# Scores of twelve tiles in PSUM, and ScalarE scaling a copy for the leaky step, in the plain layers of a graph attention network

## The chip, the cores and the metric

The kernel runs on one core of a Trainium2 chip. The metric is the device time of one execution in microseconds (us). Five engines work side by side: TensorE (PE, matmuls and weight loads), VectorE (DVE), ScalarE (ACT), GpSimd (POOL) and SyncE (SP). They meet only at semaphores: an instruction raises a counter when it ends, another engine waits for a value of it. SBUF is the large on-chip memory; PSUM is the memory that TensorE writes to, in banks of 512 float32 per partition, which DVE and ScalarE can read and write too and GpSimd can't.

## The reference, cut to what matters

12,500 nodes with 64 features and 212,500 edges, sorted by destination. One attention layer with two heads and edge features comes first, then three plain layers, which the change is about. Each of the three computes this (ReLU between them, a residual behind the last):

```python
def _gat_conv(x, src, dst, W, a_src, a_dst, b, n_nodes):
    h = x @ W
    alpha_s = h @ a_src
    alpha_d = h @ a_dst
    e = alpha_s[src] + alpha_d[dst]
    e = jnp.where(e > 0, e, NEG_SLOPE * e)
    m = jax.ops.segment_max(e, dst, num_segments=n_nodes)
    m = jnp.where(jnp.isfinite(m), m, 0.0)
    ex = jnp.exp(e - m[dst])
    s = jax.ops.segment_sum(ex, dst, num_segments=n_nodes)
    alpha = ex / (s[dst] + 1e-16)
    out = jax.ops.segment_sum(alpha[:, None] * h[src], dst, num_segments=n_nodes)
    return out + b
```

NEG_SLOPE is 0.2; the leaky step is max(0.2 e, e).

## The kernel before

A plain layer cuts the edges into units of up to 2048 edges that fall on a window of 128 nodes. A unit is 16 tiles of 128 edges: an edge is a partition of a tile, a node is a column. Its scores are a block of 128 partitions x 16 tiles x 128 nodes, in which only the column of an edge's own node counts; the rest is pushed to about minus 2 to the 80th. Each layer has 116 units. The loop body holds four units (RING), and most buffers exist four times or twice. The order of work on each engine is written out by hand in one function per engine; nothing schedules it. A helper, `step`, makes DVE wait for its own instruction before it goes on (its bookkeeping shows as line 122).

For unit n, line numbers in brackets:

- GpSimd gathers the source rows of tiles 4 to 15, one indirect DMA per tile, twelve a unit (L2149). It waits only for the buffer to be free and for the indices, so that it may run up to three units ahead. Tiles 0 to 3 come from rows near the window, picked out by matmuls with one-hot matrices (L2429, L2433), which DVE makes (the picks, L2220 and L2222).
- TensorE spreads the distance of every edge's destination to every column over four PSUM banks, `ps_apart`, with four matmuls of 512 columns (L2418), and the nodes' own attention term over a row (L2410). DVE turns both into a mask in SBUF (L2204). This is done one unit ahead: the distances of unit n + 2 are spread while unit n is worked on.
- ScalarE writes the scores, one activation per tile, from mask and gathered row into `prob` in SBUF (L2362): tiles 0 to 11, then, when the last gathers have landed, 12 to 15.
- DVE takes the maximum over tiles: tiles 0 to 3 against 4 to 7 (L2276), against 8 to 11 (L2277), and, once all are scored, against 12 to 15 (L2279), then L2280 and L2281 down to one column maximum per node. Two small steps for the running sums follow (L2250, L2255), then the leaky step over the whole block (L2285).
- Meanwhile TensorE transposes the column maximum (L2489), spreads distances, and adds up tiles 8 to 11 of the unit before (L2463). DVE reduces (L2289), applies slope and the running maximum (L2290, L2292); TensorE transposes the result (L2494, L2495). DVE subtracts it from the scores (L2299, three pieces), ScalarE takes the exponential (L2392), TensorE adds up (L2463). The result of the unit two before is projected for the next layer (L2450, ScalarE's copy L2348, L2442), except in the last layer, where it is stored with a residual (L2243).

## Time and profile before

| | us |
|---|---|
| median of 3 runs | 8424.12 (8423.76 to 8430.99) |
| profiled execution, its own time | 8423.76 |
| its span, first to last instruction | 8421.8 |
| busy: DVE | 7298.0 (87%) |
| busy: POOL | 6249.3 (74%) |
| busy: PE | 6174.9 (73%) |
| busy: ACT | 4528.2 (54%) |
| granted TensorE clock, mean | 0.614 of 2.4 GHz |

Busy time is the time in which an engine has an instruction of its own under way; issuing and waiting are not in it. The three plain layers lie from about 2540 us to the end, the two-headed layer and the preparation ahead of them. Shares over the whole span mix these parts, so the rows below are taken from stretches of the plain layers. A releaser, written behind an arrow, is what the profile takes to have ended a wait.

### The profile page before, as it was taken

What the parts mean: (1) busy time and instruction counts of PE and PEld (TensorE: products, weight loads), DVE (VectorE), ACT (ScalarE), POOL (GpSimd) and SP (SyncE); (2) the same over time, 40 slices, a digit from 0 to 9 for tenths busy, and PEclk for the clock granted to TensorE, in tenths of its full rate; (3) what the DMA queues carried; (4) which work ended last, traced back from release to release, by engine and by line L of the source; (5) the groups of instructions that cost most, each with busy time, mean ns of one, the idle gap of its engine ahead of it and who ended that gap; (6) DMA issues with size and microseconds to landing.
All of it is one profiled execution on the core that took longest, in us unless ns stands there. A gap on an engine that the chain in (4) does not pass through costs nothing. (4 is left out here: it accounts for less than half of the span.)

```text
span 8421.8 us, 166392 instructions
## 1 busy us (share of the span) xinstructions
PE 6174.9 (73%) x42912; PEld 5513.0 (65%) x42912; DVE 7298.0 (87%) x15865; ACT 4528.2 (54%) x13224; POOL 6249.3 (74%) x5871
## 2 busy tenths in 40 slices
PE   3666766677766777777777887777776777777777
PEld 3666656666655666666666776666665666666666
DVE  7888888888888888888887888888888888888888
ACT  3777767777754555454554444444444444444444
POOL 5777767777727777777776777777776777777776
PEclk9666666666666656555655556565555555555555
DMA  3222222222222222222222222222222222222222
GB/s 92 51 54 51 52 49 55 51 55 59 57 76 49 38 37 38 37 38 38 37 38 39 37 38 38 37 38 38 37 38 40 41 42 42 41 42 42 41 42 37
DMA packets 599846, 379.87 MB, mean 45 GB/s; under 512 B 435012, under 2 KB 488015, under 8 KB 599478
## 3 DMA queue, kind: packets, MB, share of 16 engines
q0 software_dynamic: 187248, 203.53, 14.9%
q1 hardware_dynamic: 404561, 169.88, 8.9%
q10 hardware_dynamic: 7952, 5.60, 0.2%
q14 instruction: 66, 0.54, 0.0%
q8 instruction: 19, 0.31, 0.0%
HBM read 345.43 MB, written 33.90 MB: 45 GB/s over the span
## 5 line engine op out<-in xcount | busy, mean ns | idle before, releaser
L2149 POOL DMA_INDIRECT plain_rows_in<-table,plain_idx x4176 | 4521.7, 1083 | 1401.9 <-issue 1386.1
L2463 PEld LDWEIGHTS plain_ps_sums<-plain_rows_in,plain_prob 128*128 128x128 f32 x11232 | 2241.0, 297 | 183.6 <-issue 66.0
L2463 PE MATMUL plain_ps_sums<-plain_rows_in,plain_prob 128*128 128x65 f32 x11232 | 2265.9, 381 | 31.0 <-ACT plain_prob L2392 20.8
L2392 ACT ACTIVATE plain_prob<-plain_prob 128x512 f32<-128x512 f32 (+1 forms) x1044 | 795.0, 772 | 2635.2 <-DVE plain_prob L2299 2593.8
L1517 POOL DMA_INDIRECT heads_rows_in<-h_in,heads_idx x1664 | 1702.8, 1023 | 655.0 <-issue 586.5
L2362 ACT ACTIVATE plain_prob<-plain_mask,plain_rows_in 128x128 f32<-128x128 f32 x5568 | 1684.0, 388 | 236.9 <-DMA plain_rows_in<-table,plain_idx 197.6
L2299 DVE TENSOR_TENSOR plain_prob<-plain_prob,plain_ps_max 128x512 f32<-128x512 f32 (+1 forms) x1044 | 841.1, 861 | 321.4 <-PE plain_ps_max L2495 321.4
L2433 PEld LDWEIGHTS plain_ps_out<-plain_pieces,plain_picks 128*128 128x128 bf16 x15795 | 956.2, 136 | 0.0
L2433 PE MATMUL plain_ps_out<-plain_pieces,plain_picks 128*128 128x66 bf16 x15795 | 939.6, 245 | 0.0
L2204 DVE SCALAR_TENSOR_TENSOR plain_mask<-plain_ps_apart,plain_er_rows 128x2048 f32<-128x2048 f32 x351 | 804.5, 2292 | 16.4 <-PE plain_ps_apart L2418 4.3
L2285 DVE SCALAR_TENSOR_TENSOR plain_prob<-plain_prob 128x2048 f32<-128x2048 f32 x348 | 795.8, 2287 | 0.0
L1832 PE MATMUL heads_ps_turn<-ident,heads_onehot 128*128 128x128 f32 x1680 | 346.9, 375 | 565.4 <-ACT heads_pairs_t L1710 434.6
L1758 ACT ACTIVATE heads_masked<-heads_mask,heads_scores_sum 128x128 f32<-128x128 bf16 x2496 | 748.8, 389 | 0.0
L1832 PEld LDWEIGHTS heads_ps_turn<-ident,heads_onehot 128*128 128x128 f32 x1680 | 276.1, 194 | 589.9 <-issue 452.2
L2429 PE MATMUL plain_ps_out<-plain_own,plain_self_pick 128*128 128x66 f32 x702 | 238.8, 444 | 574.0 <-DVE plain_picks L2222 563.0
L2410 PE MATMUL plain_ps_max<-ident,plain_er_wide 128*128 128x128 f32 x354 | 139.7, 395 | 679.1 <-DVE plain_column_max L2281 616.1
L2429 PEld LDWEIGHTS plain_ps_out<-plain_own,plain_self_pick 128*128 128x128 f32 x702 | 175.8, 311 | 637.5 <-DVE plain_picks L2222 312.9
L2418 PE MATMUL plain_ps_apart<-selector,plain_dst_local 128*128 128x512 bf16 x1416 | 575.8, 551 | 0.0
L2410 PEld LDWEIGHTS plain_ps_max<-ident,plain_er_wide 128*128 128x128 f32 x354 | 59.1, 167 | 766.8 <-issue 766.8
L1853 PEld LDWEIGHTS heads_ps_acc<-heads_weighted,heads_onehot 128*128 128x128 f32 x3328 | 535.4, 255 | 14.2 <-issue 14.2
L1853 PE MATMUL heads_ps_acc<-heads_weighted,heads_onehot 128*128 128x130 f32 x3328 | 536.3, 336 | 11.0 <-DVE heads_weighted L1634 11.0
L2222 DVE TENSOR_SCALAR plain_picks<-plain_locs,block_ids 128x384 bf16<-128x384 f16 x1755 | 452.1, 322 | 0.0
(385 smaller groups left out, 9812.4 us busy)
## 6 DMA issues: line engine op xcount, KB each, us to landing
plain_rows_in<-table,plain_idx POOLq DMA_INDIRECT x4176
heads_edges<-in_edge_attr SPq DMA_DIRECT2D x108, 512.0 KB
plain_locs<-arranged_loc SPq DMA_DIRECT2D x360, 128.0 KB
heads_rows_in<-h_in,heads_idx POOLq DMA_INDIRECT x1664
plain_own<-table SPq DMA_DIRECT2D x360, 33.5 KB
table<-plain_out_sb SPq DMA_DIRECT2D x232, 33.5 KB
plain_dst_ids<-arranged_dst SPq DMA_DIRECT2D x360, 8.0 KB
plain_unit_par<-plain_floats SPq DMA_DIRECT2D x360, 1.0 KB
```

Of the source, the lines that this page charges most:

```text
L1517: gp.indirect_dma_start(rows_in[h][:, t, :], None, table[:, :], bass.IndirectOffsetOnAxis(ap=idx[h][:, t:t + 1], axis=0)).then_inc(gathere ...
L1758: ins = ac.activation(tile, mask[:, t, :], ACT.Identity, bias=scores_sum[:, t, hd:hd + 1])
L1832: ins = te.transpose(ps_turn[g % TURN_BANKS][0:NB, t % GROUP * P:(t % GROUP + 1) * P], onehot[h][:, t, :], con.ident[:, :])
L1853: ins = te.matmul(acc_ps, onehot[h][:, t, :], weighted[:, t, :], start=t == 0, stop=t == Q - 1)
L2149: gp.indirect_dma_start(rows_in[h][:, t, :], None, table[:, :], bass.IndirectOffsetOnAxis(ap=idx[h][:, t - KEPT:t - KEPT + 1], axis=0)).th ...
L2204: ve.scalar_tensor_tensor(mask[h % 2][:, :, :], apart, 0.0, bcast(er_rows[:, :], 1, Q), ALU.not_equal, ALU.subtract).then_inc(mask_made, 1)
L2285: step(ve.scalar_tensor_tensor(tile[:, :, :], tile[:, :, :], SLOPE, tile[:, :, :], ALU.mult, ALU.max))
L2299: ve.tensor_tensor(tile[:, cols, :], tile[:, cols, :], bcast(max_row, 1, count), ALU.subtract).then_inc(logits_made, 1)
L2362: ins = ac.activation(prob[h % 2][:, t, :], mask[h % 2][:, t, :], ACT.Identity, bias=rows_in[h][:, t, src_at:src_at + 1], scale=-BIG)
L2392: ac.activation(prob[h % 2][:, cols, :], prob[h % 2][:, cols, :], ACT.Exp).then_inc(weights_made, 1)
L2433: ins = te.matmul(ps_class[:, c + 1, :], picks[h % 2][:, b, c * P:(c + 1) * P], pieces[:, k, c * BLOCKS + b, :], start=b + k == 0, stop=b ...
L2463: ins = te.matmul(sums[h % 2], prob[h % 2][:, t, :], rows_in[slot][:, t, 0:part], start=t == 0, stop=t == Q - 1)
```

## The change

Tiles 0 to 3 are scored as before. The scores of tiles 4 to 15 are written to PSUM instead, over the distances (`scores` is a second name for `ps_apart`; the four banks hold tiles 0 to 3, 4 to 7, 8 to 11 and 12 to 15). DVE takes the maxima out of them with one input in PSUM. The leaky step is split: DVE does tiles 0 to 3 in SBUF as before (512 elements), between the second and the third maximum. For tiles 4 to 15 ScalarE copies the scores, multiplied by the slope, into the mask, which is no longer needed (two copies of 1024 and 512 elements); DVE takes the maximum of copy and scores (1536 elements) into `prob`. Since scores now lie over the distances, ScalarE may write them only when DVE has made the next unit's mask, and TensorE may spread the distances that come after only when DVE has taken the scores: bank 0 is spread where all four were, banks 1 and 2 behind the adding up of tiles 8 to 11 of the unit before, bank 3 behind the projection. Three semaphores are new: `tops_made` (second and third maximum), `shrunk` (copies) and `scores_taken`.

```diff
-                    step(ve.tensor_tensor(top[:, :, :], tile[:, 0:THIRD, :], tile[:, THIRD:2 * THIRD, :], ALU.max))
-                    step(ve.tensor_tensor(top[:, :, :], top[:, :, :], tile[:, 2 * THIRD:3 * THIRD, :], ALU.max))
+                    step(ve.tensor_tensor(top[:, :, :], tile[:, 0:KEPT, :], scores[:, KEPT:2 * KEPT, :], ALU.max))
+                    ve.tensor_tensor(top[:, :, :], top[:, :, :], scores[:, 2 * KEPT:EARLY, :], ALU.max
+                                     ).then_inc(tops_made, 1)
+                    step(ve.scalar_tensor_tensor(tile[:, 0:KEPT, :], tile[:, 0:KEPT, :], SLOPE, tile[:, 0:KEPT, :],
+                                                 ALU.mult, ALU.max))
                     ve.wait_ge(scored, n + 1)
-                    step(ve.tensor_tensor(top[:, :, :], top[:, :, :], tile[:, 3 * THIRD:Q, :], ALU.max))
+                    ve.wait_ge(tops_made, 2 * n + 1)
+                    ve.tensor_tensor(top[:, :, :], top[:, :, :], scores[:, EARLY:Q, :], ALU.max).then_inc(tops_made, 1)
+                    ve.wait_ge(tops_made, 2 * n + 2)
                     step(ve.tensor_tensor(top[:, 0:2, :], top[:, 0:2, :], top[:, 2:4, :], ALU.max))
...
                     make_shift(i + (h == RING - 1), after(h))
-                    step(ve.scalar_tensor_tensor(tile[:, :, :], tile[:, :, :], SLOPE, tile[:, :, :],
-                                                 ALU.mult, ALU.max))
+                    ve.wait_ge(shrunk, 2 * n + 2)
+                    ve.tensor_tensor(tile[:, KEPT:Q, :], mask[h % 2][:, KEPT:Q, :], scores[:, KEPT:Q, :], ALU.max
+                                     ).then_inc(scores_taken, 1)
...
                     ve.wait_ge(max_turned, n + 1)
+                    ve.wait_ge(scores_taken, n + 1)
...
                     for t in tiles:
-                        ins = ac.activation(prob[h % 2][:, t, :], mask[h % 2][:, t, :], ACT.Identity,
+                        raw = prob[h % 2] if t < KEPT else scores
+                        ins = ac.activation(raw[:, t, :], mask[h % 2][:, t, :], ACT.Identity,
                                             bias=rows_in[h][:, t, src_at:src_at + 1], scale=-BIG)
...
                         score(h, range(0, KEPT))
+                        ac.wait_ge(mask_made, n + 2)
...
                         score(h, range(EARLY, Q)).then_inc(scored, 1)
+                        ac.wait_ge(scored, n + 1)
+                        for k, cols in enumerate((slice(KEPT, EARLY), slice(EARLY, Q))):
+                            ac.wait_ge(tops_made, 2 * n + k + 1)
+                            ac.activation(mask[h % 2][:, cols, :], scores[:, cols, :], ACT.Copy, scale=SLOPE
+                                          ).then_inc(shrunk, 1)
...
                         te.transpose(maxima, column_max[:, :], con.ident[:, :]).then_inc(maxima_turned, 1)
-                        spread_apart(n + 2, h)
+                        te.wait_ge(local_made, n + 3)
+                        te.wait_ge(mask_made, n + 2)
+                        spread(h, [0])
                         aggregate(n, before(h), h - 1, range(HALF, REST))
 
+                        te.wait_ge(scores_taken, n + 1)
+                        spread(h, [BANK, 2 * BANK])
                         te.wait_ge(max_made, n + 1)
...
                         project(n)
+                        spread(h, [3 * BANK]).then_inc(apart_made, 1)
                         aggregate(n, before(h), h - 1, range(REST, Q))
```

`spread(h, starts)` is the matmul of L2418 for the banks in `starts`. The changed kernel has its own line numbers, some 3 to 21 higher.

DVE, one unit, from the first maximum to the reduce, before (without the bookkeeping rows of line 122 that stand between them):

```order
L2276 TENSOR_TENSOR plain_top<-plain_prob 128x512
L2277 TENSOR_TENSOR plain_top<-plain_top,plain_prob 128x512
L2279 TENSOR_TENSOR plain_top<-plain_top,plain_prob 128x512
L2280 TENSOR_TENSOR plain_top<-plain_top 128x256
L2281 TENSOR_TENSOR plain_column_max<-plain_top 128x128
L2250 TENSOR_TENSOR plain_acc_in<-plain_self_row,plain_ps_sums 128x65
L2255 TENSOR_SCALAR plain_shift_mat<-lag,plain_unit_par 128x128
L2285 SCALAR_TENSOR_TENSOR plain_prob<-plain_prob 128x2048
L2289 TENSOR_REDUCE plain_max_unit<-plain_ps_max 128x1
```

and after the change:

```order
L2279 TENSOR_TENSOR plain_top<-plain_prob,plain_ps_apart 128x512
L2280 TENSOR_TENSOR plain_top<-plain_top,plain_ps_apart 128x512
L2282 SCALAR_TENSOR_TENSOR plain_prob<-plain_prob 128x512
L2285 ISA
L2286 TENSOR_TENSOR plain_top<-plain_top,plain_ps_apart 128x512
L2287 REGISTER_ALU
L2288 TENSOR_TENSOR plain_top<-plain_top 128x256
L2289 TENSOR_TENSOR plain_column_max<-plain_top 128x128
L2253 TENSOR_TENSOR plain_acc_in<-plain_self_row,plain_ps_sums 128x65
L2258 TENSOR_SCALAR plain_shift_mat<-lag,plain_unit_par 128x128
L2294 TENSOR_TENSOR plain_prob<-plain_mask,plain_ps_apart 128x1536
L2298 TENSOR_REDUCE plain_max_unit<-plain_ps_max 128x1
```

The 2048-element step has gone from ahead of the reduce; a 512-element one stands ahead of the third maximum, together with one sequencer instruction (ISA), and a maximum over 1536 elements ahead of the reduce.

TensorE, one unit, from the distances to the weighted sums, before:

```order
L2418 MATMUL plain_ps_apart<-selector,plain_dst_local 128x512 x4
L2462 REGISTER_ALU
L2463 MATMUL plain_ps_sums<-plain_rows_in,plain_prob 128x65 x4
L2494 MATMUL plain_ps_max<-plain_max_wide,plain_shift_mat 128x1
L2495 MATMUL plain_ps_max<-ident,plain_max_wide 128x128
L2442 MATMUL plain_ps_out<-plain_ext_wx,plain_result_t 128x66
L2463 MATMUL plain_ps_sums<-plain_rows_in,plain_prob 128x65 x4
```

and after the change, from the first distance matmul:

```order
L2432 MATMUL plain_ps_apart<-selector,plain_dst_local 128x512
L2483 REGISTER_ALU
L2484 MATMUL plain_ps_sums<-plain_rows_in,plain_prob 128x65 x4
L2432 MATMUL plain_ps_apart<-selector,plain_dst_local 128x512 x2
L2519 MATMUL plain_ps_max<-plain_max_wide,plain_shift_mat 128x1
L2520 MATMUL plain_ps_max<-ident,plain_max_wide 128x128
L2463 MATMUL plain_ps_out<-plain_ext_wx,plain_result_t 128x66
L2432 MATMUL plain_ps_apart<-selector,plain_dst_local 128x512
L2484 MATMUL plain_ps_sums<-plain_rows_in,plain_prob 128x65 x4
```

One distance matmul is left ahead of the weighted sums of the unit before, two stand directly ahead of the maximum's transposes (L2519 and L2520, before L2494 and L2495), and one behind the projection.

ScalarE, one unit of the changed kernel, from the scores in PSUM to the copy of the result:

```order
L2373 ACTIVATE plain_ps_apart<-plain_mask,plain_rows_in 128x128 x8
L2398 ISA
L2373 ACTIVATE plain_ps_apart<-plain_mask,plain_rows_in 128x128 x4
L2402 ISA
L2403 ACTIVATE plain_mask<-plain_ps_apart 128x1024
L2402 REGISTER_ALU
L2403 ACTIVATE plain_mask<-plain_ps_apart 128x512
L2358 ACTIVATE plain_result_t<-plain_ps_out 64x128
```

The two copies into the mask stand behind the last scores and ahead of the copy of the result, which before came directly behind the scores.

## Rows read from the trace of the kernel before

**Rows 1.** windows, mask line L2204 alone, five stretches: us, DVE busy (count), PEclk, DMA, GB/s

```profile
2561.30:2951.00 389.70, 55.01 (x24) 0.63 0.22 38
2951.00:4466.00 1515.00, 208.59 (x91) 0.59 0.22 38
4540.50:4931.00 390.50, 55.01 (x24) 0.58 0.23 38
4931.00:6429.00 1498.00, 206.29 (x90) 0.59 0.22 38
6481.30:8392.00 1910.70, 263.58 (x115) 0.57 0.24 42
```

**Rows 2.** waits of DVE in stretches 1, 2, 4, 5: us, times, longest

```profile
DVE plain_prob L2299 <- PE plain_ps_max L2495: 18.6, 24, 1.3
DVE plain_prob L2299 <- PE plain_ps_max L2495: 81.7, 91, 1.3
DVE plain_top L2279 <- ACT plain_prob L2362: 39.4, 59, 0.9
DVE plain_prob L2299 <- PE plain_ps_max L2495: 113.4, 115, 1.3
```

**Rows 3.** instruction groups, POOL, stretch 4: busy, mean ns, idle and its releasers

```profile
L2149 POOL DMA_INDIRECT plain_rows_in<-table,plain_idx x1081 | 1170.1, 1082 | 329.4 <-issue 329.4
```

**Rows 4.** timeline, a unit of layer two: start, us, instruction, idle before

```profile
5340.19 2.29 DVE L2285 SCALAR_TENSOR_TENSOR plain_prob<-plain_prob 128x2048 f32<-128x2048 f32 x1
5341.41 1.89 POOL L2149 DMA_INDIRECT plain_rows_in<-table,plain_idx  x1 [0.30 <-issue]
5344.44 2.42 DVE L2299 TENSOR_TENSOR plain_prob<-plain_prob,plain_ps_max 128x512 f32<-128x512 f32 x3 [0.92 <-PE plain_ps_max L2495]
5344.85 0.94 POOL L2149 DMA_INDIRECT plain_rows_in<-table,plain_idx  x1 [0.30 <-issue]
5346.78 0.31 DVE L2196 TENSOR_SCALAR plain_dst_local<-plain_dst_ids,plain_unit_par 16x128 bf16<-16x128 int32 x1
```

**Rows 5.** instruction groups by form, DVE, stretch 5

```profile
L2285 DVE SCALAR_TENSOR_TENSOR plain_prob<-plain_prob 128x2048 f32<-128x2048 f32 x115 | 262.9, 2286 | 0.0
L2299 DVE TENSOR_TENSOR plain_prob<-plain_prob,plain_ps_max 128x512 f32<-128x512 f32 x230 | 147.8, 684 | 113.4 <-PE plain_ps_max L2495 113.4
L2299 DVE TENSOR_TENSOR plain_prob<-plain_prob,plain_ps_max 128x1024 f32<-128x1024 f32 x115 | 139.6, 1214 | 0.0
L2277 DVE TENSOR_TENSOR plain_top<-plain_top,plain_prob 128x512 f32<-128x512 f32 x115 | 79.6, 692 | 3.9
```

**Rows 6.** timeline, third layer, the unit at 7007

```profile
7005.65 0.69 DVE L2279 TENSOR_TENSOR plain_top<-plain_top,plain_prob 128x512 f32<-128x512 f32 x1
7007.50 2.28 DVE L2285 SCALAR_TENSOR_TENSOR plain_prob<-plain_prob 128x2048 f32<-128x2048 f32 x1
7010.68 0.38 PE L2494 MATMUL plain_ps_max<-plain_max_wide,plain_shift_mat 128*128 128x1 f32 x2 [1.20 <-DVE plain_max_wide L2292]
7011.34 1.28 DVE L2299 TENSOR_TENSOR plain_prob<-plain_prob,plain_ps_max 128x512 f32<-128x512 f32 x2 [0.52 <-PE plain_ps_max L2495]
```

**Rows 7.** timeline, third layer, the unit at 6923

```profile
6924.05 1.91 PE L2418 MATMUL plain_ps_apart<-selector,plain_dst_local 128*128 128x512 bf16 x4
6925.75 1.81 PE L2463 MATMUL plain_ps_sums<-plain_rows_in,plain_prob 128*128 128x65 f32 x8
6928.31 2.42 DVE L2299 TENSOR_TENSOR plain_prob<-plain_prob,plain_ps_max 128x512 f32<-128x512 f32 x3 [1.25 <-PE plain_ps_max L2495]
```

**Rows 8.** instruction groups by form, ACT, heads layer

```profile
L1758 ACT ACTIVATE heads_ps_masked<-heads_mask,heads_scores_sum 128x128 f32<-128x128 bf16 x744 | 230.3, 356 | 157.5 <-DVE heads_scores_sum L1567 155.2
L1710 ACT ACTIVATE heads_pairs_t<-heads_ps_turn 128x512 f32<-128x512 f32 x186 | 98.1, 576 | 0.0
```

**Rows 9.** timeline, a unit of layer two, scores and the first maximum

```profile
6014.49 3.62 ACT L2362 ACTIVATE plain_prob<-plain_mask,plain_rows_in 128x128 f32<-128x128 f32 x12
6018.77 0.69 DVE L2276 TENSOR_TENSOR plain_top<-plain_prob 128x512 f32<-128x512 f32 x1 [0.16 <-DVE plain_self_row L2269]
```

More of the change, by code:

```diff
@@ L1987, in plain_layer @@
         apart = ps_apart[:, 0:CAP].rearrange("p (t n) -> p t n", n=NB)
+        scores = ps_apart[:, 0:CAP].rearrange("p (t n) -> p t n", n=NB)
         max_row = ps_max[:, MROW_AT:MROW_AT + NB]
@@ L2010, in plain_layer @@
         scored_early, scored = sem("scored_early"), sem("scored")
+        shrunk, scores_taken = sem("shrunk"), sem("scores_taken")
+        tops_made = sem("tops_made")
         columns_maxed, maxima_turned = sem("columns_maxed"), sem("maxima_turned")
@@ L2165, in _ @@
                 rounds = unit_rounds(ve)
-                STEPS = 18
+                STEPS = 16
                 ve.tensor_copy(idx[0][:, :], con.first_idx[:, :]).then_inc(first_copied, 1)
@@ L2410, in turn_er, with spread @@
                     te.transpose(er_row, er_wide[:, :], con.ident[0:NB, 0:NB]).then_inc(er_turned, 1)
+                def spread(h, starts):
+                    for at in starts:
+                        ins = te.matmul(ps_apart[:, at:at + BANK], dst_local[h % 2][:, :], selector[:, at:at + BANK])
+                    return ins
                 def spread_apart(n, h):
@@ L2416, in spread_apart @@
                         te.wait_ge(mask_made, n)
-                    for at in range(0, CAP, BANK):
-                        ins = te.matmul(ps_apart[:, at:at + BANK], dst_local[h % 2][:, :], selector[:, at:at + BANK])
-                    ins.then_inc(apart_made, 1)
+                    spread(h, range(0, CAP, BANK)).then_inc(apart_made, 1)
                 def pick_rows(n, k, slot, h):
```

## The prediction, made before the changed kernel had run

> **What bounds the kernel now.** I read the count of one instruction per layer first, then the waits, then single units, then durations.
>
> Each unit of the three plain layers builds one mask, so the mask line's count gives the pace [rows 1]. In the first layer the first 24 units take 389.7 / 24 = 16.24 us each and the next 91 take 16.65; in the second it is 16.27, then 16.64; in the third 1910.7 / 115 = 16.61 throughout. Two regimes, then. In the slower stretches VectorE (DVE) waits for ScalarE's last scores, 39.4 us over 59 of 90 units [rows 2], and GpSimd's gathers never wait for anyone: 1081 of them at 1082 ns and 329.4 / 1081 = 0.30 us of issue each make 1.39 us, twelve a unit 16.6 us, which is the pace itself [rows 3] to 0.1 us. There the gathers set the pace; the first units of a layer live on gathers made ahead. In the third layer DVE has one wait of weight, for the transposed maximum, 113.4 / 115 = 0.99 us a unit [rows 2], and none for scores: DVE sets the pace.
>
> Why a gather takes 1.08 us: undisturbed it takes 0.94. The one issued at 5341.41, while the leaky step of 2048 elements runs, takes 1.89 and ends 0.82 us after DVE is done. The one issued while L2299 runs (one input in PSUM) takes 0.94 [rows 4]. So DVE instructions with two SBUF inputs hold gathers up. This stands against a rule: the Trainium skill (SBUF — State Buffer, section Who interferes with whom) lets a two-SBUF-input instruction contend with GpSimd's reads, but infers that tensor_tensor takes only the read side, and so does not stall descriptor generation. The rows disagree, at least where the gather reads its indices. By that inference nothing is freed; rival C below has its time, from rows.
>
> **The change, part by part** (per unit, 116 units in each of three layers).
>
> 1. Gathers. The leaky step on 2048 elements and the three maxima over 512 stop having two SBUF inputs, except for a leaky step over 512 (0.69 us). Undisturbed gathers need 12 x (0.94 + 0.30) = 14.9 us; were one held by the whole 0.69 us and another by the two small maxima, 15.9. Both are under 16.2, so gathers no longer set the pace. Worth at most 91 x (16.65 - 16.24) + 90 x (16.64 - 16.27) = 37 + 33 = 70 us. The first 24 units of layer one had a shorter wait for the maximum (18.6 / 24 = 0.78 against 81.7 / 91 = 0.90 us [rows 2]), and PE's clock is higher in that row, 0.63; that 0.12 x 91 = 11 us isn't mine. And 3 us go back for the second layer the other way. I take -62 us; ends 0 (rival C) and -70.
>
> 2. DVE before the column maximum. Added: a leaky step over 512. A 2048 one takes 2286 ns; 1536 elements less by the slope of L2299 (530 ns per 512) leave 0.69 us [rows 5]. It needn't wait for the maximum in front of it: independent instructions start 0.08 us before the one ahead ends (L2196 begins at 5346.78, L2299 ends at 5346.86 [rows 4]), so it adds 0.69 - 0.08 = 0.61. Behind it the third maximum has one more sequencer instruction in front, as the order shows (ISA). No row has this: L2277, with a plain wait for its predecessor, starts 3.9 / 115 = 0.03 us after it [rows 5]; L2276, which has a semaphore increment in between, 0.16 [rows 9]. So 0 to 0.13; I take 0.08. The maxima themselves: one PSUM input, L2299's 684 ns against 692 ns [rows 5], -0.02. Sum +0.67. It is hidden only where scores are late, and after part 1 they aren't. The Trainium skill (Perfetto Trace Analysis, section Optimizing Scalar/DVE Operations) gives DVE about 60 ns of access overhead on SBUF and 125 on PSUM. By it the three maxima and the 1536 instruction would cost 0.26 us more a unit, and the whole would come out some 90 us slower; the 684 and 692 ns speak against it.
>
> 3. DVE behind the column maximum. The 2048 leaky step (2.29) goes, a maximum over 1536 with one PSUM input comes: 684 + 2 x 530 = 1.74. The reduce no longer waits for it, another 0.03 + 0.08. So the maximum over the unit is ready 0.65 earlier. How much of that arrives depends on PE. In the unit at 7007 PE has waited 1.20 us for DVE when the maximum comes, and DVE then waits 0.52 [rows 6]: all 0.65 arrives, if the two distance matmuls now standing between fit; at PE's pace there they do. In the unit at 6923 the four distance matmuls take 1.91 us, PE is behind and DVE waits 1.25 [rows 7]. There DVE's gain is worth nothing and only PE's order counts: three distance matmuls instead of four stand ahead of the maximum's transposes, and one is worth 0.43 (four in 1.71 between starts, 6924.05 to 6925.75). The mean wait in layer three, 0.99 [rows 2], lies 64% of the way from 0.52 to 1.25. But two slow matmuls (0.85) behind the taken scores would outlast the roughly 0.8 us of DVE's work that remain there, should the clock be low at just that point: as a choice, I count half of the fast ones at 0.43. So -(0.64 x 0.43 + 0.18 x 0.65 + 0.18 x 0.43) = -0.47; ends -0.43 and -0.65.
>
> 4. ScalarE. Twelve scores go to PSUM. In the heads layer a 128x128 activation into PSUM takes 356 ns [rows 8], into SBUF here 0.30 from start to start [rows 9], and nothing in the row speaks for a dearer one. The first four may start as before; the next eight wait for the next unit's mask, done by then in the unit shown, and the scores are there 0.66 us before DVE asks (18.11 against 18.77 [rows 9]). The two copies, 0.58 us for 512 elements out of PSUM [rows 8] and under twice that for 1024, run beside DVE. The second must be done before the 1536 instruction: it may start when the third maximum ends, 7006.34, and is asked for at 7007.50 [rows 6], 1.16 later, with some 0.7 needed if 0.1 is allowed for the signal. Free, with 0.45 to spare. The result's copy slips behind them; its projection comes after the maximum's transposes, later still. PE's last distance matmul, behind the projection, has the 2.42 us of L2299 [rows 4] to end in before DVE asks for it.
>
> Sum: parts 2 and 3, +0.67 - 0.47 = +0.20 us, x 348 = +70; with a little overlap lost back in layer one (every fourth unit there ScalarE reloads a table and DVE waits anyway) I take +66. With -62: **+4 us**, on the profiled execution's 8423.8 (the median of the runs is 8424.1): **8428 us**.
>
> **Rivals.**
>
> A, faster: DVE's additions are cheaper than I say. If every unit behaves as the one of rows 6 (0.65 arrives) and the extra sequencer instruction costs nothing, the adder is 0.59 - 0.65 = -0.06, -21 us in all: 8424 - 62 - 21 = 8341. Half way, adder 0.07: 8386. For: clock 0.63 where units were shortest [rows 1]; against: 0.57 in the third layer. I give it 8388.
>
> B, slower than before: PE decides. Where the clock is low, -0.43 is all that part 3 gives. If PE is behind in all units and the sequencer costs 0.13, the adder is 0.72 - 0.43 = 0.29, +101 us, less 62: 8463. It is slower from the point where the adder passes 62 / 348 = 0.18 us; beyond 0.23 it can be measured. For: the third layer's 64% and the narrow fit of the two matmuls; against: DVE's 0.65 did have room at 7007.
>
> C, the gathers aren't freed (they are held by any DVE instruction, or by ScalarE's copies into the mask): the slow stretches keep 16.65 us and swallow the adder in their wait; the other 48 + 116 units pay 0.20: +33, 8457. Against: rows 4.
>
> D, a new wait on ScalarE: from 0.45 us more for the copies, or 0.08 us more for each of the eight scores, it shows, and each 0.1 us beyond is 35 us. At 0.3 beyond: 8530. Against: 356 ns [rows 8].
>
> **Numbers.** What a measurement can tell from no change is 0.2%, 17 us. My forecast, adder between 0.13 and 0.25, 0.42: 8407 to 8450, mostly inside the bound (0.34 inside, 0.08 above). A 0.31, mostly faster. B 0.15, C 0.06, D 0.06, slower. Chances: faster 0.31, same 0.35, slower 0.34. Range 8375 to 8485: A's half-way case and B and C lie in it, A's end and D out.
>
> **What would show it.** Gathers near 0.95 us everywhere, and the two regimes of layers one and two gone, each at about 16.45 us: part 1 right. Third layer at 16.8 us: parts 2 and 3 right; at 16.55 rival A, at 16.9 B. The gap ahead of the third maximum gives the sequencer's price. DVE's wait for the transposed maximum should rise from 0.99 to about 1.15, since DVE gets there earlier than PE. DVE waiting for the copies, or for the early scores, would be D; gathers at 1.08 us would be C. I am wrong about the whole if the third layer doesn't get slower at all.

## The result, and the profile after

| | before | after |
|---|---|---|
| median of the runs, us (lowest to highest) | 8424.1 (8423.8 to 8431.0) | 8485.8 (8481.5 to 8487.7) |
| ratio to before, 95% interval | 1 | 1.0071 [1.0053, 1.0088] |
| span of the profiled execution, us | 8421.8 | 8479.5 |

The change makes the kernel 0.7% slower, 62 us, where I had forecast +4 us. The median lies at the upper end of my range of 8375 to 8485, 0.8 us above it, and on the side of rival B.

The pace first: the mask line L2207 over 115 units of each layer (us, busy and count of DVE in that line, PEclk, DMA share, GB/s).

```profile
2560.20:4485.60 1925.40, 263.59 (x115) 0.54 0.23 37
4542.00:6449.80 1907.80, 263.60 (x115) 0.55 0.23 38
6503.55:8449.45 1945.90, 263.58 (x115) 0.52 0.23 41
```

The same stretches of the kernel before, the first two of them here whole, where [rows 1] had them in two pieces:

```profile
2561.30:4466.70 1905.40, 263.59 (x115) 0.60 0.22 38
4523.85:6429.40 1905.55, 263.59 (x115) 0.59 0.22 38
```

After: 16.74, 16.59 and 16.92 us a unit, against 16.57, 16.57 and 16.62 before (the last from [rows 1]). That is +20, +2 and +35 us for the layers, 57 of the 62 us lost. Beside each stands a lower granted clock. All layers are slower, the third most.

Groups of the page after, in the order busy, mean ns, idle before and its releasers:

```profile
L2152 POOL DMA_INDIRECT plain_rows_in<-table,plain_idx x4176 | 4021.5, 963 | 1949.8 <-issue 1355.2
L2373 ACT ACTIVATE plain_ps_apart<-plain_mask,plain_rows_in 128x128 f32<-128x128 f32 x4176 | 1239.8, 350 | 0.0
L2309 DVE TENSOR_TENSOR plain_prob<-plain_prob,plain_ps_max 128x512 f32<-128x512 f32 (+1 forms) x1044 | 841.3, 861 | 433.3 <-PE plain_ps_max L2520 433.3
L2294 DVE TENSOR_TENSOR plain_prob<-plain_mask,plain_ps_apart 128x1536 f32<-128x1536 f32 x348 | 608.3, 1748 | 0.0
```

The gathers went from 1082 ns [rows 3] to 963, and now they wait for buffers: 594.4 of the 1949.8 us of idle time end with PE's sums (L2484). So they have time to spare. The scores cost 350 ns each, the 1536 maximum 1748, both as forecast. What stands out is 433.3 us of waiting for the transposed maximum, 1.25 us a unit (1.32 in the third layer, where I had expected 1.15). DVE's waits between 2600 and 8300 us (us, times, longest) show nothing else of weight: the 301 short ones are the 0.16 us ahead of the first maximum, as before, and no wait is for ScalarE's copies.

```profile
DVE plain_prob L2309 <- PE plain_ps_max L2520: 417.9, 336, 1.4
DVE plain_top L2279 <- DVE plain_self_row L2272: 48.3, 301, 0.7
DVE plain_top L2279 <- ACT plain_ps_apart L2373: 19.7, 29, 0.9
```

A unit of the third layer, timeline of DVE, PE and one gather (start, us, instruction, idle before), which answers to [rows 6, 7]:

```profile
7003.83 0.29 DVE L2289 TENSOR_TENSOR plain_column_max<-plain_top 128x128 f32<-128x128 f32 x1
...
7004.49 1.75 DVE L2294 TENSOR_TENSOR plain_prob<-plain_mask,plain_ps_apart 128x1536 f32<-128x1536 f32 x1
...
7004.91 0.94 POOL L2152 DMA_INDIRECT plain_rows_in<-table,plain_idx  x1 [0.30 <-issue]
...
7005.24 1.81 PE L2484 MATMUL plain_ps_sums<-plain_rows_in,plain_prob 128*128 128x65 f32 x8 [0.22 <-issue]
...
7006.15 0.28 DVE L2298 TENSOR_REDUCE plain_max_unit<-plain_ps_max 128x1 f32<-128x128 f32 x1
...
7006.67 0.29 DVE L2301 TENSOR_TENSOR plain_max_wide<-plain_max_before,plain_max_unit 128x128 f32<-128x128 f32 x1
...
7006.84 1.06 PE L2432 MATMUL plain_ps_apart<-selector,plain_dst_local 128*128 128x512 bf16 x2
...
7007.69 0.42 PE L2519 MATMUL plain_ps_max<-plain_max_wide,plain_shift_mat 128*128 128x1 f32 x2
...
7007.98 0.45 PE L2520 MATMUL plain_ps_max<-ident,plain_max_wide 128*128 128x128 f32 x1
...
7008.52 2.42 DVE L2309 TENSOR_TENSOR plain_prob<-plain_prob,plain_ps_max 128x512 f32<-128x512 f32 x3 [1.37 <-PE plain_ps_max L2520]
```

DVE has the maximum ready at 7006.96. PE is still behind: it ends the sums of the unit before, then does the two distance matmuls, and turns to the maximum only at 7007.69. DVE had read the scores out of their banks by 7006.24, so that in this unit they waited for PE alone. DVE stands idle for 1.37 us. The granted clock here is 0.50, the 1.2 GHz level.

Three stretches of a unit show where the time went (means over the units of a layer, from the timelines of DVE, before to after):

| us a unit | layer one | layer two | layer three |
|---|---|---|---|
| first maximum to column maximum | 2.86 to 3.32 | 2.98 to 3.32 | 2.65 to 3.32 |
| column maximum to the subtraction (L2299, L2309) | 4.87 to 4.58 | 4.90 to 4.52 | 4.98 to 4.64 |
| subtraction to the next first maximum | 8.84 to 8.83 | 8.69 to 8.73 | 8.99 to 8.95 |

In the first row, layers one and two of the kernel before hold 0.22 and 0.34 us of waiting for late scores (L2279); those waits are gone after.

### The profile page after: what moved, and what is told of

The parts are those of the page before. It is cut to its first block and busy times, and to the rows that moved or that the text cites. A ratio compares the mean times of both kernels' runs of the same rounds, so it can differ in the third digit from the quotient of the medians.

```text
span 8479.5 us, 167694 instructions
## 1 busy us (share of the span) xinstructions
PE 6324.5 (75%) x42561; PEld 5787.7 (68%) x42912; DVE 7289.0 (86%) x16213; ACT 5041.4 (59%) x13920; POOL 5748.8 (68%) x5871
## 5 line engine op out<-in xcount | busy, mean ns | idle before, releaser
L2152 POOL DMA_INDIRECT plain_rows_in<-table,plain_idx x4176 | 4021.5, 963 | 1949.8 <-issue 1355.2
L2484 PEld LDWEIGHTS plain_ps_sums<-plain_rows_in,plain_prob 128*128 128x128 f32 x11232 | 2462.6, 321 | 86.6 <-ACT plain_prob L2409 2.9
L2484 PE MATMUL plain_ps_sums<-plain_rows_in,plain_prob 128*128 128x65 f32 x11232 | 2382.5, 400 | 66.3 <-issue 59.8
L2373 ACT ACTIVATE plain_ps_apart<-plain_mask,plain_rows_in 128x128 f32<-128x128 f32 x4176 | 1239.8, 350 | 0.0
L2309 DVE TENSOR_TENSOR plain_prob<-plain_prob,plain_ps_max 128x512 f32<-128x512 f32 (+1 forms) x1044 | 841.3, 861 | 433.3 <-PE plain_ps_max L2520 433.3
L2403 ACT ACTIVATE plain_mask<-plain_ps_apart 128x1024 f32<-128x1024 f32 (+1 forms) x696 | 564.2, 811 | 537.8 <-DVE plain_top L2280 399.4
L2207 DVE SCALAR_TENSOR_TENSOR plain_mask<-plain_ps_apart,plain_er_rows 128x2048 f32<-128x2048 f32 x351 | 804.5, 2292 | 16.2 <-PE plain_ps_apart L2432 4.2
L2294 DVE TENSOR_TENSOR plain_prob<-plain_mask,plain_ps_apart 128x1536 f32<-128x1536 f32 x348 | 608.3, 1748 | 0.0
```

What stands on the lines that cost most here:

```text
L2152: gp.indirect_dma_start(rows_in[h][:, t, :], None, table[:, :], bass.IndirectOffsetOnAxis(ap=idx[h][:, t - KEPT:t - KEPT + 1], axis=0)).th ...
L2207: ve.scalar_tensor_tensor(mask[h % 2][:, :, :], apart, 0.0, bcast(er_rows[:, :], 1, Q), ALU.not_equal, ALU.subtract).then_inc(mask_made, 1)
L2309: ve.tensor_tensor(tile[:, cols, :], tile[:, cols, :], bcast(max_row, 1, count), ALU.subtract).then_inc(logits_made, 1)
L2373: ins = ac.activation(raw[:, t, :], mask[h % 2][:, t, :], ACT.Identity, bias=rows_in[h][:, t, src_at:src_at + 1], scale=-BIG)
L2484: ins = te.matmul(sums[h % 2], prob[h % 2][:, t, :], rows_in[slot][:, t, 0:part], start=t == 0, stop=t == Q - 1)
```

## The experiments

All medians are of runs beside runs of the kernel before. Paces are us a unit, taken as above.

| kernel | median us | ratio, interval | pace by layer | clock by layer |
|---|---|---|---|---|
| before | 8424.1 | 1 | 16.57, 16.57, 16.62 | .60 .59 .57 |
| after | 8485.8 | 1.0071 [1.0053, 1.0088] | 16.74, 16.59, 16.92 | .54 .55 .52 |
| e1_step_late | 8227.6 | 0.9765 [0.9749, 0.9781] | 15.99, 15.90, 16.17 | .55 .55 .54 |
| e4_step_behind_max | 8355.6 | 0.9911 [0.9895, 0.9928] | 16.39, 16.30, 16.52 | .55 .54 .54 |
| e2_spread_late | 8343.1 | 0.9902 [0.9885, 0.9918] | 16.31, 16.12, 16.61 | .57 .57 .54 |
| e3_both | 8094.8 | 0.9607 [0.9591, 0.9623] | 15.60, 15.43, 15.87 | .56 .57 .54 |
| b1_spread_late_before | 8333.6 | 0.9891 [0.9874, 0.9907] | 16.29, 16.10, 16.57 | .57 .57 .54 |
| b3_sbuf_split_only | 8413.0 | 0.9984 [0.9974, 0.9993] | 16.43, 16.49, 16.54 | .60 .58 .56 |
| b2_sbuf_both | 8390.9 | 0.9963 [0.9949, 0.9977] | 16.43, 16.46, 16.25 | .56 .56 .54 |
| g1_eleven_gathers | 8350.2 | 0.9909 [0.9892, 0.9925] | 16.32, 16.22, 16.62 | .61 .58 .57 |
| e5_used_later | 8090.4 | 0.9597 [0.9583, 0.9610] | 15.60, 15.50, 15.76 | .57 .56 .54 |

**The leaky step over 512, moved.** From the kernel after; the step goes from between the second and third maximum to behind the rescale, into DVE's wait for the transposed maximum.

```diff
-    step(ve.scalar_tensor_tensor(tile[:, 0:KEPT, :], ..., SLOPE, ...))   # after the 2nd maximum
...
     step(ve.tensor_tensor(rescale[h][:, :], max_before[:, :], max_wide[:, 0:1], ALU.subtract))
+    step(ve.scalar_tensor_tensor(tile[:, 0:KEPT, :], ..., SLOPE, ...))
```

> The changed kernel, with the 512-element leaky step moved from ahead of the third maximum to the place behind the rescale step, where DVE waits for the transposed maximum (1.37 us in most units, 0.86 in the others). Theory (DVE pays 0.68 us ahead of the column maximum, and what it saves behind it ends in a wait for TensorE): the third maximum starts 0.04 instead of 0.82 us after the second, the wait falls by 0.7 in the slow units, the unit gets shorter by 0.6 to 0.7 us, 348 units by 210 to 245: 8240 to 8275 us, faster than both kernels. Rival (TensorE's queue, with its lower granted clock, sets the pace of the whole unit): under 0.2 us a unit, above 8410. Rival (ScalarE's copies or scores become late): DVE's wait shows up at the third maximum or the 1536-element maximum, and the gain is under half.

258 us less than after, a little more than I expected, and the wait fell from 433.3 us to 151.2 over 240 units. 258 / 348 = 0.74 us a unit: the whole price of the added step went, 0.70 of it between first and column maximum, and the stretch behind the column maximum did not get longer by the step (4.51, 4.51 and 4.59 us). So the wait is real room, and the step's place ahead of the column maximum was what the change paid with.

Halfway, with the same step just ahead of the wait for `shrunk`, behind the column maximum (the maximum's way over PE starts earlier, but DVE still does the step before it reduces):

> The changed kernel, with the 512-element step directly ahead of the 1536-element maximum, so behind the column maximum but not in the wait for the transposed one. Theory: the 0.72 us ahead of the column maximum go; behind it TensorE is late anyway where its clock is low (85% of the units), and DVE's 0.61 more there cost only some 0.1, since the two distance matmuls wait for scores_taken; at full clock they cost all: about 0.5 us a unit, 8290 to 8330, that is more than e1_step_late's 8228. Rival (where DVE's step stands doesn't matter as long as DVE is busy): 8480.

It gained 130 us, half of the 258, less than I expected. The 0.70 us ahead of the column maximum went, but 0.33 came back behind it; the wait for the transposed maximum is 297.6 us, 0.86 in nearly every unit.

**PE's order.** From the kernel after; no distance matmul stands between the transposes of the two maxima except the first.

```diff
-    te.wait_ge(scores_taken, n + 1)
-    spread(h, [BANK, 2 * BANK])
     ... # transposes of the maximum, projection
-    spread(h, [3 * BANK]).then_inc(apart_made, 1)
+    te.wait_ge(scores_taken, n + 1)
+    spread(h, [BANK, 2 * BANK, 3 * BANK]).then_inc(apart_made, 1)
```

> The changed kernel, with the distance matmuls of banks 1 and 2 behind the projection too, beside bank 3. Theory: in slow units TensorE then waits for the maximum instead of coming late, the transposed maximum is there 3.75 instead of 4.41 us behind the column maximum, in the others 3.75 instead of 3.90; mean 0.55 us, 348 units 190 us: about 8290. DVE's wait falls from 1.25 to 0.7. Rival (the place of two matmuls doesn't matter, the clock does): unchanged, 8485 within 20.

143 us less than after. The wait is now 298.1 us over 348 units, 0.86 in nearly every one. I had expected a shorter wait (0.7) and 8290 us: what is left is the way itself, at the low clock. From the running maximum (L2292 before, L2301 after) to the subtraction the granted clock was at the low level, 0.50 to 0.55, in 199 of the 348 units before, in 327 after and in all 348 of e2_spread_late.

> Both edits together. Theory: the 0.73 us of the leaky step and the wait of about 0.7 just cover each other; unit 16.85 - 0.72 - 0.55 = 15.6 us, where the gathers (12 x 1.27 = 15.2) come close to setting the pace; 8040 to 8100 us. If TensorE's queue is the limit: above 8250.

Both together give 391 us, all of 258 + 143 = 401 but ten. DVE's waits between 2600 and 8000 us, and the gathers there:

```profile
DVE plain_top L2279 <- DVE plain_self_row L2272: 49.3, 311, 0.2
DVE plain_top L2279 <- ACT plain_ps_apart L2373: 25.8, 30, 0.9
...
DVE plain_prob L2309 <- PE plain_ps_max L2518: 6.5, 27, 0.5
```

```profile
L2152 POOL DMA_INDIRECT plain_rows_in<-table,plain_idx x4092 | 3911.7, 956 | 1490.3 <-issue 1380.5 <-PE plain_ps_sums L2484 109.8
```

The wait of 433 us is gone, and a unit shows why: the 512 step lies where the wait was.

```profile
5212.31 0.29 DVE L2299 TENSOR_TENSOR plain_max_wide<-plain_max_before,plain_max_unit 128x128 f32<-128x128 f32 x1
...
5212.66 0.59 PE L2517 MATMUL plain_ps_max<-plain_max_wide,plain_shift_mat 128*128 128x1 f32 x2
5212.87 0.69 DVE L2303 SCALAR_TENSOR_TENSOR plain_prob<-plain_prob 128x512 f32<-128x512 f32 x1
5213.11 0.45 PE L2518 MATMUL plain_ps_max<-ident,plain_max_wide 128*128 128x128 f32 x1
...
5213.65 2.42 DVE L2309 TENSOR_TENSOR plain_prob<-plain_prob,plain_ps_max 128x512 f32<-128x512 f32 x3
```

**Is it the PSUM scores at all?** The same two rearrangements on the kernel before, with scores in SBUF: first PE's order alone.

```diff
-    spread_apart(n + 2, h)              # four matmuls ahead of the maximum's transposes
+    te.wait_ge(local_made, n + 3); te.wait_ge(mask_made, n + 2)
+    spread(h, [0])
     ... # sums, transposes of the maximum, projection
+    spread(h, [BANK, 2 * BANK, 3 * BANK]).then_inc(apart_made, 1)
```

> The kernel before, with TensorE's order changed alone: one distance matmul ahead of the weighted sums of the unit before, three behind the projection. Theory (gathers set the pace in the later nine tenths of layers one and two, DVE and TensorE in the third): the transposed maximum comes 4.25 to 4.4 instead of 4.69 us behind the column maximum; third layer 0.35 us a unit, 40 us; the first 24 units of the other layers 14 us; the rest of them nothing: 8370 us, and their pace stays at 16.65. Rival (gathers never set the pace): all 348 units gain, 8300.

A miss: 90 us gained, not 54, and in the wrong layers: 0.28 and 0.47 us a unit in layers one and two, where I held that the gathers set the pace at 16.65, and only 0.05 in the third, which I held to be DVE's. Most of the gain lies between first and column maximum, 2.64 us in both layers: the 0.22 and 0.34 us of waiting for late scores are gone here too, with the scores still in SBUF. The gathers took 1054 ns in the mean: how often a gather is held depends on where it falls beside DVE's steps, so their pace is no constant of the kernel. In the third layer PE's clock fell (low in the round trip in 115 of 116 units, 85 before), and DVE waited 0.87 us in nearly all units instead of 0.72 in the mean of one half and 1.25 in the other: 0.12 us gained behind the column maximum, and 0.08 lost in the rest of the unit.

Then the leaky step split as well: 1536 columns where it was, 512 behind the rescale.

```diff
-    step(ve.scalar_tensor_tensor(tile[:, :, :], tile[:, :, :], SLOPE, ...))
+    step(ve.scalar_tensor_tensor(tile[:, KEPT:Q, :], tile[:, KEPT:Q, :], SLOPE, ...))
...
+    step(ve.scalar_tensor_tensor(tile[:, 0:KEPT, :], tile[:, 0:KEPT, :], SLOPE, ...))   # behind the rescale
```

> The kernel before, scores all in SBUF, with both edits of e3_both: TensorE's three distance matmuls behind the projection, and the leaky step split into 1536 elements where it was and 512 behind the rescale step. DVE and TensorE then do what they do in e3_both (15.6, 15.4 and 15.9 us a unit in the three layers); what differs is that six DVE instructions have two SBUF inputs. Theory (those hold the gathers up, by 1.2 to 1.6 us a unit, on top of 12 x 1.25 = 15.0): the gathers set the pace at 16.2 to 16.5 us in all layers, 8290 to 8370 us. Rival (the gathers' stalls are harmless, and scores in PSUM bring nothing): 8095 within 25.

> The kernel before with the leaky step split alone, TensorE's order as it was. Theory: in units at low clock TensorE brings the maximum 4.95 us behind the column maximum whatever DVE does, and the 512 elements fill its wait: nothing; at full clock 0.5 us; the third layer some 0.2 us a unit, the gathers hold the other two at about 16.6: 8395 to 8425. Rival (DVE alone sets the pace): 0.7 us in each unit of the third layer and of the first 24 of the others, 8310.

The runs of these two spread more than the others (8355 to 8411, 8388 to 8428), and each was profiled in its fastest, so their paces flatter them. The split alone (b3_sbuf_split_only) brings 0.2%, as expected. With DVE's and PE's order arranged alike, SBUF scores take 8390.9 us (slower than I expected) and PSUM scores 8094.8. The difference, 296 us, is what the scores' place is worth in this order of work. It is not the distance to the best kernel with SBUF scores: that is b1_spread_late_before with 8333.6, 239 us behind e3_both. There the small leaky step in the round trip does harm: in b2_sbuf_both 300 of the 345 gathers that begin inside it are held. With SBUF scores the gathers bind, group of the page of b2_sbuf_both and DVE's wait in it between 2600 and 8300 us:

```profile
L2149 POOL DMA_INDIRECT plain_rows_in<-table,plain_idx x4176 | 4464.6, 1069 | 1404.3 <-issue 1404.0
```

```profile
DVE plain_top L2279 <- ACT plain_prob L2364: 169.1, 222, 1.1
```

GpSimd waits for nothing there, and DVE waits for late scores in 222 units. The timeline shows a gather held beside the leaky step, which has both inputs in SBUF, and one not held beside the mask, which has one in PSUM. It is so in every unit: all 345 gathers that begin inside this leaky step over 1536 are held, and so are all 344 that begin inside the one over 2048 of the kernel before; of the 695 that begin inside the mask there, none is.

```profile
5239.88 2.29 DVE L2204 SCALAR_TENSOR_TENSOR plain_mask<-plain_ps_apart,plain_er_rows 128x2048 f32<-128x2048 f32 x1
5240.52 0.94 POOL L2149 DMA_INDIRECT plain_rows_in<-table,plain_idx  x1 [0.30 <-issue]
...
5250.14 1.76 DVE L2285 SCALAR_TENSOR_TENSOR plain_prob<-plain_prob 128x1536 f32<-128x1536 f32 x1
5251.35 1.36 POOL L2149 DMA_INDIRECT plain_rows_in<-table,plain_idx  x1 [0.30 <-issue]
```

**One gather less.** The kernel before without the gathers of tile 4 (its edges are left out), eleven a unit.

```diff
-    for t in range(KEPT, Q):
+    for t in range(KEPT + 1, Q):
```

> The kernel before with eleven gathers a unit instead of twelve in the plain layers; tile 4 of each buffer holds what was written once, so its edges are left out of the sums. Theory: the pace of layers one and two falls from 16.57 on average to the 16.2 to 16.3 of their first units, the third layer stays at 16.62: 8424 - 62 = 8362, within 15. If the gathers don't set the pace anywhere: 8424. If they held all three layers up: the third gets shorter too.

As expected: 74 us, from layers one and two (0.25 and 0.35 us a unit), and nothing in the third. This confirms what part 1 of the forecast rested on, the 70 us that less work for GpSimd is worth in the kernel as it was.

**The increment ahead of the first maximum.**

```diff
-    ve.sem_inc(unit_used, 1)          # ahead of the first maximum
...
+    ve.sem_inc(unit_used, 1)          # behind the column maximum
```

> The kernel of e3_both with one DVE instruction moved: the increment of unit_used, which stands between the sixteenth tile's step and the first maximum, goes right behind the column maximum, where the trace of e3_both has other small gaps anyway. Theory: an instruction of the sequencer alone between two dependent steps costs 0.12 us (gaps of 0.16 us ahead of the first maximum in e3_both against 0.03 to 0.04 between two plain steps), and nothing waits for unit_used at that point: the gap goes from 0.16 to about 0.04, 348 units give 42 us, so 8053 us, within 10. Rival 1: the gap belongs to the maximum's own wait for its semaphore and not to the increment; then the gap stays 0.16 and the time stays at 8095, within 10. Rival 2: DVE does not set the pace of a unit in e3_both; then the gap goes but a wait elsewhere takes the place, and the time stays at 8095.

The gap went as the theory has it, the time did not: about 8 us by the ratios, whose intervals overlap, not 42. It is, with e3_both, 4% faster than the kernel before. Groups between 2600 and 8000 us, of e3_both and then of e5_used_later (count, busy, mean ns):

```profile
L2225 DVE TENSOR_SCALAR plain_picks<-plain_locs,block_ids 128x384 bf16<-128x384 f16 x1710 | 439.6, 324 | 0.0
L2258 DVE TENSOR_SCALAR plain_shift_mat<-lag,plain_unit_par 128x128 f32<-128x128 f32 x343 | 109.0, 318 | 12.0
L2279 DVE TENSOR_TENSOR plain_top<-plain_prob,plain_ps_apart 128x512 f32<-128x512 f32 x341 | 234.4, 688 | 75.1 <-DVE plain_self_row L2272 49.3 <-ACT plain_ps_apart L2373 25.8
```

```profile
L2225 DVE TENSOR_SCALAR plain_picks<-plain_locs,block_ids 128x384 bf16<-128x384 f16 x1715 | 473.9, 340 | 0.0
L2258 DVE TENSOR_SCALAR plain_shift_mat<-lag,plain_unit_par 128x128 f32<-128x128 f32 x343 | 122.1, 356 | 12.4 <-DVE plain_acc_in L2253 0.5
L2278 DVE TENSOR_TENSOR plain_top<-plain_prob,plain_ps_apart 128x512 f32<-128x512 f32 x340 | 233.8, 688 | 33.4 <-ACT plain_ps_apart L2373 22.6
```

49.3 us of gaps went, and picks and shift took 34 + 13 us more at the same count: five picks at 16 ns and one shift at 38 give 0.12 us a unit back. Why these small steps stretch (their phase beside the gathers, whose mean went from 956 to 981 ns, changed) was not tried and is left open.

## Where the prediction was right, and where it went wrong

**What bounds the kernel: right, in two regimes,** though not as fixed as I had it. g1_eleven_gathers shows that layers one and two of the kernel before lose to the gathers what I said and the third nothing. b1_spread_late_before shows that PE's order moves the same layers, so "the gathers set the pace at 16.65" holds for one phase only.

**Part 1, the gathers: right in mechanism and in size.** 963 ns, against "near 0.95"; of the 462 gathers that begin inside the 1536 maximum none is held (the one at 7004.91 above runs its 0.94). The two regimes of layers one and two are gone (16.79 and 16.73 us a unit, 16.63 and 16.58), and so are the waits for late scores, 0.22 x 115 + 0.34 x 115 = 64 us, against my 62. Rival C is out. What is not shown is that the freed gathers alone took these waits away: b1_spread_late_before lost them by PE's order, with gathers of 1054 ns. The Trainium skill (SBUF — State Buffer, section Who interferes with whom) infers that tensor_tensor, even with two SBUF inputs, does not stall GpSimd's descriptor generation. That does not hold here: 120 of the 212 gathers that begin inside the first maximum of the kernel before (L2276, a tensor_tensor with two SBUF inputs) end about 0.82 us after it instead of after their own 0.94.

**Part 2, +0.67 ahead of the column maximum: right.** From the first maximum to the column maximum a unit of the third layer takes 0.68 us more; in layers one and two it is 0.46 and 0.34, since the waits for scores went there. The 512 step starts 0.61 behind the second maximum's start, and the third maximum 0.81 behind that: 0.69 and a gap of 0.13 (median), where the kernel before has 0.03. The sequencer instruction so costs 0.10, for which I had taken 0.08:

```profile
7018.28 0.69 DVE L2280 TENSOR_TENSOR plain_top<-plain_top,plain_ps_apart 128x512 f32<-128x512 f32 x1
...
7018.89 0.69 DVE L2282 SCALAR_TENSOR_TENSOR plain_prob<-plain_prob 128x512 f32<-128x512 f32 x1
...
7019.70 0.69 DVE L2286 TENSOR_TENSOR plain_top<-plain_top,plain_ps_apart 128x512 f32<-128x512 f32 x1
```

**Part 3, -0.47 behind it: this is the step that failed,** the term "-(0.64 x 0.43 + 0.18 x 0.65 + 0.18 x 0.43)". It measured -0.29, -0.38 and -0.34 in the three layers. That what arrives depends on whether PE is behind was right; that the change leaves PE behind in as many units as before was not. Read off the timelines of the 115 units of the third layer, the time from the column maximum's start to the subtraction falls into two groups, told apart by DVE's wait. In the units with a wait of 1.2 us or more PE is behind, and the granted clock over that time was 0.50 in every one; in the others it was 0.73 in the mean before and 0.62 after:

| third layer | units with wait of 1.2 or more | the others | mean |
|---|---|---|---|
| before | 57, 5.25 us | 58, 4.71 us | 4.98 |
| after | 98, 4.70 us | 17, 4.31 us | 4.64 |

Within the groups the gain is 0.55 and 0.40 us. Had the groups kept their sizes of before, it would be 0.5 x 0.55 + 0.5 x 0.40 = 0.48. That this is my 0.47 is luck: I had weighed the units with PE behind at 0.64, which were 0.50, and priced them at 0.43, where they brought 0.55, and the others at 0.54, where they brought 0.40. But 41 units moved from the short group to the long one: 41 / 115 x (4.70 - 4.31) = 0.14 us a unit, and the gain was 0.34. In the first layer the long group went from 34 to 84 units, in the second from 44 to 67, worth (4.70 - 4.25) x 50 / 115 = 0.20 and (4.71 - 4.26) x 23 / 115 = 0.09. Together 0.43 x 115 = 49 us of the 58 that I missed by. A unit that went from the short group (4.71) to the long one (4.70) gained nothing behind the column maximum, and had the 0.68 ahead of it to pay in full. A unit of the short group, after, in which the first transpose still ran fast (0.30):

```profile
5282.24 0.30 PE L2427 MATMUL plain_ps_max<-ident,plain_er_wide 128*128 128x128 f32 x1 [1.88 <-DVE plain_column_max L2289]
...
5284.18 1.04 PE L2432 MATMUL plain_ps_apart<-selector,plain_dst_local 128*128 128x512 bf16 x2 [0.47 <-DVE plain_prob L2294]
...
5285.01 0.48 PE L2519 MATMUL plain_ps_max<-plain_max_wide,plain_shift_mat 128*128 128x1 f32 x2
5285.35 0.46 PE L2520 MATMUL plain_ps_max<-ident,plain_max_wide 128*128 128x128 f32 x1
...
5285.89 2.42 DVE L2309 TENSOR_TENSOR plain_prob<-plain_prob,plain_ps_max 128x512 f32<-128x512 f32 x3 [0.86 <-PE plain_ps_max L2520]
```

Here PE has caught up and waits 0.47 us for the scores to be taken; only then may the two distance matmuls start. They outlast DVE's reduce, and by then the clock has fallen (0.70 granted over 5282 to 5286): the two transposing steps take 0.48 and 0.46, where [rows 6] has 0.38 for the first. This is the "narrow fit" that I had counted for half of the fast units. PE waited for the scores in 42 of the 96 units of the short groups of the three layers, but in all 96 the maximum's transposes started 0.76 to 0.85 us behind the first of the two distance matmuls, the slow pace (0.43 each at the low level) or near it. DVE's wait is 0.86 there, where [rows 6] has 0.52.

I had taken the granted clock, and so the groups, as unchanged. It fell from .60, .59, .57 to .54, .55, .52. The table of the experiments shows with what it goes: kernels with PE's order of before have .60, .58, .56 or more, whatever DVE does and however many gathers there are (b3, g1); those with the distance matmuls late have .56 or .57, and .54 in the third, with scores in SBUF or PSUM (b1, b2, e2, e3, e5); those with PE's order of after have .54 or .55 in layers one and two (after, e1, e4). b1_spread_late_before changes nothing but PE's order and moves it by 0.02 to 0.03. So PE's order goes into the clock, and the groups, which go with the clock, moved; what in it does (the order of the kinds of matmuls, or how its idle time is cut up) stays open.

**Part 4, ScalarE: right.** No wait of DVE is for the copies (1.02 and 0.60 us, [rows 8] gave 0.58), and those for early scores are no longer than before (20.1 us in all, 25.8 before). Rival D is out.

**The sum.** Part 2 came at its price and part 1 too; part 3 fell short by 0.13 us a unit in the mean, 46 us of the 58. Of the rest, 4 us are the overlap that I had taken off the sum (66 for 70), about 5 lie outside the units of the three layers, and 3 are part 2's 0.68 against 0.67. Rival B came nearest: it had PE behind in all units and 8463, and by my own sign the third layer's 16.92 us speaks for it. What it lacked is that PE would get slower itself: it gave every unit 0.43, also those that were not behind before.

## What to carry to other kernels

Freeing a shared resource pays only when the steps that the change adds don't land on the path that was second: here what the scores' place is worth was spent on one 0.69 us step in front of a round trip, and two matmuls inside it. Put added work into the wait of the round trip, and keep work that can be late out of it; the four corners (8424 and 8391 with SBUF scores, 8486 and 8095 with PSUM scores, as ordered first and with both rearrangements) show that the two ideas bring far more together, 329 us, than the scores' place (62 us lost) or the rearrangements (33 us) alone. Of the rearrangements PE's order alone is worth more with SBUF scores (90 us, b1_spread_late_before) than both. And where units fall into two groups by TensorE's granted clock, forecast the groups' sizes too: a new order on PE changes them.

## What the runs showed of the hardware that I had not expected

- The granted clock of TensorE moved with the order of its instructions, at the same count of them: .60 to .57 in layer one by moving three matmuls of each unit (b1_spread_late_before), .54 in the kernel after.
- One instruction for DVE's sequencer alone, between dependent steps, costs 0.10 to 0.12 us where it has to wait for the step ahead itself (gaps of 0.13 and 0.16 against 0.03 to 0.04), and it goes away when the instruction moves (e5_used_later). In e3_both the instruction that cost 0.10 after stands between the second and third maximum, runs while the second is under way, and the gap is 0.03.
- An indirect gather that begins while DVE's leaky step works with two sources in SBUF is held until about 0.82 us after DVE is done (5251.35 to 5252.71, DVE done at 5251.90), for a step of 1536 as for one of 2048. One that begins shortly before the step is not: 344 gathers of the kernel before began up to 0.83 us ahead of it, and none took over 0.99.
- DVE's small steps on 16-bit data are not of fixed length: the picks took 318 ns in the mean in b1_spread_late_before, 324 in e3_both and 346 in b2_sbuf_both.
